# x lands in z instead of a ring of buffers, and a rearranged last stage: wavelet, convolution and median on one NeuronCore

## Time and profile before

| | us |
|---|---|
| median of 3 runs | 419.66 (417.89 to 421.17) |
| the profiled execution | 418.86 |
| its span, first to last instruction | 417.1 |
| TensorE matmuls busy | 396.9 (95%) |
| VectorE busy | 375.6 (90%) |
| GpSimd busy | 190.8 (46%) |
| ScalarE busy | 152.9 (37%) |
| DMA moved | 26.72 MB, mean 64 GB/s |

### The profile page before, as it was taken

How to read it: one execution, slowest core, us unless ns; L and a number is a source line. 1 busy time by engine, 2 the same in 40 slices (tenths; PEclk the granted TensorE clock), 3 DMA queues, 4 the chain that set the end, 5 groups by cost and what they waited for, 6 DMA issues and landing times.

```text
span 417.1 us, 3651 instructions
## 1 busy us (share of the span) xinstructions
PE 396.9 (95%) x1120; PEld 210.5 (50%) x1120; DVE 375.6 (90%) x532; ACT 152.9 (37%) x348; POOL 190.8 (46%) x194
## 2 busy tenths in 40 slices
PE   7889999999999999999999999999999998699983
PEld 2335588856444444444444444444446787564331
DVE  3899857999849999999999998989989999999993
ACT  2565753412262432323241414141424222229902
POOL 3999395622624443445454343434343520006620
PEclk9999999999999999999999999999999999889995
DMA  8970200100101011010101001010100000002673
GB/s 301 410 320 3 95 6 2 50 0 2 51 0 50 4 47 52 0 50 0 50 2 51 27 23 50 3 50 0 51 0 2 0 1 2 0 0 116 282 282 127
DMA packets 7796, 26.72 MB, mean 64 GB/s; under 512 B 992, under 2 KB 1248, under 8 KB 7776
## 3 DMA queue, kind: packets, MB, share of 16 engines
q1 hardware_dynamic: 7776, 26.48, 16.7%
HBM read 18.09 MB, written 8.39 MB: 63 GB/s over the span
## 4 chain that ended last, share of the span: by engine, by line
PE 71%; DVE 13%; POOL 5%; ACT 5%; issue 3%; DMA 2%; SPq 0%; POOLq 0%; DVEq 0%
PE conv_ps L381 65%; ACT z L618 3%; PE one_ps L363 3%; PE one_ps L446 2%; POOL y L212 2%; POOL y L213 2%; DMA ru<-x 2%; PE conv_ps L469 1%; POOL y L340 1%; DVE one_ps L821 1%; DVE sorted_cols L792 1%; DVE sorted_cols L794 1%; DVE sorted_cols L790 1%; DVE sorted_cols L787 1%; DVE z L823 1%
## 5 line engine op out<-in xcount | busy, mean ns | idle before, releaser
L381 PE MATMUL conv_ps<-ru,wt 128*128 128x512 f32 (+1 forms) x360 | 133.7, 509 | 0.0
L381 PEld LDWEIGHTS conv_ps<-ru,wt 128*128 128x128 f32 x360 | 69.9, 195 | 53.9 <-issue 50.2
L381 PE MATMUL conv_ps<-xu,wt 128*128 128x496 f32 (+3 forms) x240 | 88.6, 506 | 5.6 <-DVE conv_ps L757 5.6
L569 ACT ACTIVATE y<-conv_ps,sgn 128x512 f32<-128x512 f32 (+1 forms) x40 | 25.5, 637 | 171.0 <-PE conv_ps L381 171.0
L381 PEld LDWEIGHTS conv_ps<-xu,wt 128*128 128x128 f32 x240 | 46.0, 193 | 42.0 <-issue 33.2
L319 POOL TENSOR_TENSOR ru<-eo 128x512 f32<-128x512 f32 x16 | 17.0, 1061 | 86.5 <-DVE one_ps L785 86.4
L219 POOL TENSOR_TENSOR ru<-z 128x512 f32<-128x512 f32 x14 | 18.1, 1290 | 59.4 <-DVE one_ps L827 59.4
L381 PE MATMUL conv_ps<-ru,v 128*128 128x496 f32 (+3 forms) x120 | 43.7, 500 | 0.0
L381 PE MATMUL conv_ps<-y,wt 128*128 128x496 f32 (+3 forms) x108 | 38.6, 491 | 0.0
L381 PE MATMUL conv_ps<-y,v 128*128 128x496 f32 (+3 forms) x108 | 38.6, 491 | 0.0
L469 PE MATMUL conv_ps<-z,w 128*128 128x512 f32 x64 | 31.2, 637 | 4.8 <-POOL z L349 4.3
(11 more groups left out here) (128 smaller groups left out, 639.8 us busy)
## 6 DMA issues: line engine op xcount, KB each, us to landing
raw<-x SPq DMA_DIRECT2D x20, 512.0 KB, 3.3
out<-y SPq DMA_DIRECT2D x15, 512.0 KB, 2.6
ru<-x SPq DMA_DIRECT2D x8, 512.0 KB, 8.7
xu<-x SPq DMA_DIRECT2D x4, 512.0 KB, 8.7
wt<-w_t SPq DMA_DIRECT2D x2, 576.0 KB, 10.6
out<-y SPq DMA_DIRECT2D x2, 256.0 KB, 2.1
w<-w_t SPq DMA_DIRECT2D x2, 64.0 KB, 4.7
vec<-vectors SPq DMA_DIRECT2D x1, 3.0 KB, 9.5
```

The lines of the kernel that those rows point to most:

```text
L381: return nc.tensor.matmul(bank(u, b)[:, (r0 - row) * BW:(r1 - row) * BW], taps(half, kx, ky), plane[:, (r0 + dy) * BW:(r1 + dy) * BW], sta ...
L569: S.activation(at(slot(n), row * W + b, [[2, cols]]), src, ACT.Identity, scale=sgn[:, :], accum_out=y_sum[:, part:part + 1]).then_inc(y_ke ...
```

## The change

- x is loaded straight into `zslot(n)`, the place of the image's bands in `z`. The ring is gone, each image has a semaphore of its own, and SyncE issues all 16 loads with no wait. The vectors and weights stay behind the eighth. All waits that guarded the ring's buffers go.
- The seeds of unit 18 move from the piece of unit 16 to the end of the piece of unit 15; those of unit 19 from the piece of unit 17 to the piece of unit 16.
- The batch norm stands behind step 7 of the last three pieces (units 17, 18, 19).
- Images 3, 6, 9 and 12 (`SUMMED`) are finished without VectorE: ScalarE maps `y` with ReLU, TensorE adds it through an identity matrix (`unit`) onto the mix, and ScalarE writes PSUM + b as output. The other twelve (`OWN`) are mapped by GpSimd and finished by VectorE; nine of them stand behind steps 16, 19, ... 40 of the last three pieces, the others behind the last piece.
- GpSimd builds the identity after its last `make_xu03`. `KEEP_WARM` is 30.

```
-    WARM_UP, KEEP_WARM = 8, 24
-    RING = 8
+    WARM_UP, KEEP_WARM = 8, 30
...
-    BN3_AT, FINISH_AT = 8, tuple(range(15, 29))
-    ACT_SHARE = 1
+    SUMMED = (3, 6, 9, 12)
+    OWN = [n for n in range(IMAGES) if n not in SUMMED]
+
+    BN3_AT, FINISH_AT = 7, (16, 19, 22, 25, 28, 31, 34, 37, 40)
...
-        ring = [raw[0], raw[1], ru03[0], ru03[1], ru12[1], ru12[0], xu03[1], xu03[0]]
+        unit = sb("unit", [CH, CH])
...
         def make_xu12(v, n):
-            src = ring[n % RING]
-            e, o = at(src[:, :], 0, [[2, HALF]]), at(src[:, :], 1, [[2, HALF]])
+            e, o = at(zslot(n), 0, [[2, HALF]]), at(zslot(n), 1, [[2, HALF]])
...
-            for n in range(RING):
-                sp.dma_start(ring[n][:, :], x_img[:, n, :]).then_inc(x_in[n], 16)
-            sp.dma_start(vec[:, :], vectors).then_inc(vec_in, 16)
-            for half in (X_HALF, R_HALF):
-                cols = slice(half * KY * KX * CH, (half + 1) * KY * KX * CH)
-                sp.dma_start(wt[:, cols], w3_cols[:, cols]).then_inc(w3_in[half], 16)
-            for n in range(RING, IMAGES):
-                sp.wait_ge(x_in[n - RING], 16)
-                wait_xu12(sp, n - RING)
-                sp.dma_start(ring[n - RING][:, :], x_img[:, n, :]).then_inc(x_in[n - RING], 16)
+            for n in range(IMAGES):
+                sp.dma_start(zslot(n), x_img[:, n, :]).then_inc(x_in[n], 16)
+                if n == 7:
+                    sp.dma_start(vec[:, :], vectors).then_inc(vec_in, 16)
+                    for half in (X_HALF, R_HALF):
+                        cols = slice(half * KY * KX * CH, (half + 1) * KY * KX * CH)
+                        sp.dma_start(wt[:, cols], w3_cols[:, cols]).then_inc(w3_in[half], 16)
...
             for n in range(IMAGES):
-                if n < 2:
-                    sp.wait_ge(x_in[n], 32)
-                    wait_xu12(sp, n + RING)
-                else:
+                if n >= 2:
...
+            G.memset(unit[:, :], 1.0).then_inc(ones_set, 1)
+            pool.wait_ge(ones_set, 1)
+            G.affine_select(out=unit[:, :], in_=unit[:, :], pattern=[[-1, CH]], base=0, channel_multiplier=1,
+                            compare_op=ALU.is_equal, fill=0.0).then_inc(unit_made, 1)
...
-                    mm = nc.tensor.matmul(conv_ps[:, k, b * BANK:(b + 1) * BANK], w2[:, :], zslot(n)[:, b * BANK:(b + 1) * BANK],
-                                          start=True, stop=True)
+                    half = slice(b * BANK, (b + 1) * BANK)
+                    mm = nc.tensor.matmul(conv_ps[:, k, half], w2[:, :], zslot(n)[:, half], start=True, stop=n in OWN)
+                    if n in SUMMED:
+                        pe.wait_ge(x1_by_act, SUMMED.index(n) + 1)
+                        mm = nc.tensor.matmul(conv_ps[:, k, half], unit[:, :], slot(n)[:, half], start=False, stop=True)
...
+            for n in range(1, IMAGES):
                 norm_median(n)
-                if n % 4 >= 4 - ACT_SHARE:
-                    map_x1(n)
+                if n in SUMMED:
+                    S.activation(slot(n), slot(n), ACT.Relu, bias=shift3[:, :], scale=scale3[:, :]).then_inc(x1_by_act, 1)
+                if n - 2 in SUMMED:
+                    act.wait_ge(mix_done, n - 1)
+                    S.activation(slot(n - 2), conv_ps[:, n % 2, :], ACT.Identity, bias=cb2).then_inc(out_by_act, 1)
...
+            EARLY, LATE = {}, {}
+            for u in range(2, len(UNITS)):
+                before = EARLY if UNITS[u - 2][0] in HALVED or UNITS[u][0] in HALVED else LATE
+                before[u - 2] = u
+            last = len(UNITS) - 1
+            del EARLY[last - 3], EARLY[last - 2]
+            LATE[last - 4], EARLY[last - 3] = last - 1, last
...
-            medians(PIECES[-2:], step_and_more)
+            medians(PIECES[-3:], step_and_more)
```

More of the change, by code:

```diff
@@ L82, in wavelet_conv_median_kernel @@
         ru03 = [sb(f"ru03_{k}", [CH, PIX]) for k in range(2)]
-        ring = [raw[0], raw[1], ru03[0], ru03[1], ru12[1], ru12[0], xu03[1], xu03[0]]
-        assert len(ring) == RING
         UP = BW + 1
@@ L124, in wavelet_conv_median_kernel @@
         tmp1, tmp2 = one_ps[:, 0, :], one_ps[:, 1, :]
-        x_in = [sem(f"x_in{k}") for k in range(RING)]
+        x_in = [sem(f"x_in{n}") for n in range(IMAGES)]
         raw_in = [sem(f"raw_in{k}") for k in range(2)]
@@ L183, in wavelet_conv_median_kernel @@
         mix_done = sem("mix_done")
+        ones_set = sem("ones_set")
+        unit_made = sem("unit_made")
+        out_by_act = sem("out_by_act")
         out_ready = sem("out_ready")
@@ L249, in _ @@
             for n in range(IMAGES - 1):
-                sp.wait_ge(out_ready, n + 1)
+                if n in SUMMED:
+                    sp.wait_ge(out_by_act, SUMMED.index(n) + 1)
+                else:
+                    sp.wait_ge(out_ready, OWN.index(n) + 1)
                 sp.dma_start(out_img[:, n, :], slot(n)).then_inc(out_sent, 16)
             for part in range(2):
-                sp.wait_ge(out_ready, IMAGES + part)
+                sp.wait_ge(out_ready, len(OWN) + part)
                 half = slice(part * HALF, (part + 1) * HALF)
@@ L279, in _ @@
             for n in BY_POOL:
-                pool.wait_ge(x_in[n % RING], 16 * (n // RING + 1))
+                pool.wait_ge(x_in[n], 16)
                 make_xu12(G, n).then_inc(xu12_by_pool, 1)
@@ L313, in make_ru03 @@
                 pool.wait_ge(eo_made, n + 1)
-                if n < 2:
-                    wait_xu12(pool, 2 + RING + n)
-                else:
+                if n >= 2:
                     pool.wait_ge(rows_read, last_unit(n - 2) + 1)
@@ L349, in _ @@
                 G.memset(at(zslot(n), 0, [[(H - 1) * W, 2], [W - 1, 2]]), 0.0).then_inc(med_ready, 1)
-                if n % 4 < 4 - ACT_SHARE:
+                if n in OWN:
                     map_x1(n)
@@ L478, in _ @@
             pe.wait_ge(w2_in, 16)
+            pe.wait_ge(unit_made, 1)
             pe.wait_ge(squares_summed, PARTS_ALL)
@@ L482, in _ @@
             for n in range(2, IMAGES):
-                pe.wait_ge(out_ready, n - 1)
+                if n - 2 in SUMMED:
+                    pe.wait_ge(out_by_act, SUMMED.index(n - 2) + 1)
+                else:
+                    pe.wait_ge(out_ready, OWN.index(n - 2) + 1)
                 mix(n, n % 2)
@@ L541, in x_edges @@
                 act.wait_ge(raw_in[k], 16 * (n // 2 + 1))
-                if n < 2:
-                    wait_xu12(act, IMAGES - 1 - n)
-                else:
+                if n >= 2:
                     act.wait_ge(y_done, 2 * (last_unit(n - 2) + 1))
@@ L618, in norm_median @@
                 S.activation(zslot(n), zslot(n), ACT.Relu, bias=shift3[:, :], scale=scale3[:, :]).then_inc(med_normed, 1)
-            def map_x1(n):
-                S.activation(slot(n), slot(n), ACT.Identity, bias=shift3_bias2[:, :], scale=scale3[:, :]).then_inc(x1_by_act, 1)
-            for n in range(1, 4):
+            for n in range(1, IMAGES):
                 norm_median(n)
-            for n in range(4 - ACT_SHARE, 4):
-                map_x1(n)
-            for n in range(4, IMAGES):
-                norm_median(n)
-                if n % 4 >= 4 - ACT_SHARE:
-                    map_x1(n)
+                if n in SUMMED:
+                    S.activation(slot(n), slot(n), ACT.Relu, bias=shift3[:, :], scale=scale3[:, :]).then_inc(x1_by_act, 1)
+                if n - 2 in SUMMED:
+                    act.wait_ge(mix_done, n - 1)
+                    S.activation(slot(n - 2), conv_ps[:, n % 2, :], ACT.Identity, bias=cb2).then_inc(out_by_act, 1)
         @block.vector
@@ L651, in split_x @@
             def split_x(n):
-                dve.wait_ge(x_in[n % RING], 16 * (n // RING + 1))
+                dve.wait_ge(x_in[n], 16)
                 make_xu12(V, n).then_inc(xu12_by_dve, 1)
@@ L731, in _ @@
                 step(V.memset(at(t, 0, [[PITCH, H + 1]]), LOW))
-            for n in range(2):
-                wait_xu12(dve, RING + 5 - n)
             for k, (normed, made) in enumerate(((first_pair_normed, first_sums_made), (bands_normed, ru12_made))):
@@ L757, in seed_odd, with median @@
                 V.tensor_tensor(q_bank, p_kept[u % 2][:, 0:cols], q_bank, ALU.subtract).then_inc(seeded, 1)
-            def median(n, kept, pair0=0, pairs=BH, step=step, seeds=None):
-                early, late = (seeds, None) if n in HALVED or n + 2 in HALVED else (None, seeds)
+            def median(n, kept, pair0=0, pairs=BH, step=step, early=None, late=None):
                 r0, nr = 2 * pair0, 2 * pairs
@@ L855, in _, with medians @@
                 done_pairs = upto
-            def medians(pieces, step=step, seeds=None):
+            EARLY, LATE = {}, {}
[5 more added lines that the diff above has]
+            LATE[last - 4], EARLY[last - 3] = last - 1, last
+            def medians(pieces, step=step):
                 for n, pair0, pairs, u in pieces:
```

(12 more changed lines are left out.)

4 lines of the change are left out of this document (1 added, 3 removed).

## The result

The changed kernel takes 417.11 us in the median of 20 runs, against 419.51 us for the kernel before, also of 20. The ratio is 0.9947, with a 95% interval from 0.9932 to 0.9961: faster by half a per cent, within the one per cent that I called no change. Two of the 20 runs took 608 and 863 us, for a reason that no kept trace shows; the ratio leaves them out.

A forecast was written before the change was run, and what follows sets the result against it. TensorE fills the convolution; VectorE's order, waiting about 3 us for TensorE's mixes, ends the kernel. Tail end 413.5 plus 0.3 for handovers gives span 413.8, profiled time 415.6, median 416.4, stated as 416.6 us; range 412.6 to 420.3.

The forecast's parts named there:

- x into z costs and brings nothing: First pass: loading x without the ring is worth 0, at worst a loss of 1 us, no gain.
- Seeds one piece earlier: Convolution's end: TensorE's pauses of 2.30 and 3.28 us vanish; unit 18 runs to 357.9 us, unit 19 to 363.1.
- Statistics: Piece of unit 17: VectorE waits 1.1 us, then works 2.4 us, to 366.7; batch norm ready 9.3 us earlier.
- what ends the kernel is VectorE's own order: Last stage: the batch norm comes 9.3 us earlier, but VectorE's own sequence of work sets the kernel's end.
- Five finishes fewer, and TensorE's 20 mixes: Last stage: last median at 402.6 us without waits; about 3 us of waits for TensorE make it 405.7, against 407.99.
- ScalarE's outputs at no cost: Last stage: ScalarE's four outputs fit beside TensorE's mixes, value 0; upper bound 0.8 us in all.
- Tail: After the last median: end at 414.8 us with the last mix at half clock, 412.8 at full; 413.5 taken.
- Rival A: Full gain: TensorE keeps its clock in the tail, VectorE waits less; times 412.5 to 415.6 us; chance 0.27.
- Rival B: No gain: TensorE's clock falls in pauses ahead of images 2 and 3, costing 1.8 us; time 419.2; chance 0.15.
- Rival C: Slower: weight changes for the sums cost TensorE 0.2 us per added matmul, 3.3 us; time 420.5; chance 0.08.
- Rival D: First pass loses image 8's margin, 1 us; chance 0.05 together with the unseen.

The follow-up runs named there:

- e8: Changed kernel with 11 warm-up matmuls in place of 8 ahead of the first image; ratio to the kernel before 0.9935.
- e1: Kernel before with only x's loads into z (no ring, none of its waits), last stage old; ratio to the kernel before 0.9997.
- e2: Changed kernel with the ring and its waits put back, last stage new; ratio to the kernel before 0.9915.
- e3: Changed kernel with SUMMED empty: early seeds and statistics stay, VectorE finishes all 16 images; ratio to the kernel before 1.0015.
- e4: Changed kernel with its four sums, but statistics back behind step 8 of unit 18's piece, later finishes, 62 keep-warm matmuls; ratio to the kernel before 0.9984.
- e6: Changed kernel with its nine finishes at earlier steps (12 to 38) and 22 keep-warm matmuls; 414.26 us, ratio to the kernel before 0.9885.
- e9: Changed kernel with earlier finishes, 22 keep-warm and 11 warm-up matmuls, image 14's mix made twice; 412.27 us, ratio to the kernel before 0.9827.
- e5: Changed kernel with three sums (images 4, 8, 12) in place of four and ten finishes behind steps 16 to 43; ratio to the kernel before 0.9936.
- e7: Changed kernel with the mix of image 14 made twice onto the same PSUM half; ratio to the kernel before 0.9939.

## Why the prediction was right

I said 416.6 us and no change within one per cent; it is 417.1. The forecast was a span 3.3 us shorter, and the mean spans differ by 3.0. The profiled execution itself came out 2.5 us longer than its forecast, 416.3 for 413.8, because the first mix and the last both ran at half clock in it. That the runs' median is only 0.5 us off owes something to luck: it hangs on how often the clock is low at these two places, and I had priced one of them with a middle value and the other not at all. In e8's profile, where neither is slow, the span is 413.6. Step by step:

- *x into z costs and brings nothing.* Right in the spans: e1, and e2 beside the changed kernel, differ from their partners by 0.2 us and by nothing. GpSimd's split of image 8 came at 19.59 us, 19.46 before. I hadn't counted the time around the span, which grew from 1.87 us in the mean to 2.35. It is 2.05 in e1 and 1.78 in e2, 1.99 to 2.46 in the others without a ring. So part of it seems to come with the new loads (eight more semaphores, for one), but no run takes that apart, and it stays open.
- *Seeds one piece earlier.* Right within 0.4 us: 15.2 us from the sums' start to the end of unit 19 (348.71 to 363.93), forecast 15.6.
- *Statistics.* Right: a wait of 1.11 us (1.1), 2.4 us of work. e3 shows that this alone is worth nothing, as the step "what ends the kernel is VectorE's own order" has it. e4 adds what I had not priced: with the sums it is worth some 2 us.
- *Five finishes fewer, and TensorE's 20 mixes.* Both sizes hold. Image 3's mix started 1.7 us later than forecast (379.37 for 377.7), and the last median ended at 407.7, 2.0 us later than 405.7. Of both, 1.2 us is the first pass (0.2 of it was won back by the first finish). Another 0.7 is a single step of the median, L781, right behind the first finish: the next instruction starts 0.97 us after it (375.48 to 376.45), where the like step at 373.99 takes 0.30. The trace shows no wait in it, and the cause stays open. In e8's profile, whose first pass isn't late, the same step is as long and the last median ends at 406.7. That VectorE loses 3 us to TensorE is borne out by e6, where nearly all of those waits are gone: its median ends at 403.4, 4.3 us sooner than in the changed kernel's profile and 3.1 sooner once that one's late first pass is taken off.
- *ScalarE's outputs at no cost.* Right: one takes 1.0 us. ScalarE idles 7.0 us ahead of the first and 1.2 ahead of each of the other three, waiting for TensorE, and TensorE has no gap behind the start of image 3's mix in which it could wait for them.
- *Tail.* I took 413.5 between full and half clock. No profile shows that: the pause of 2.3 us ends at half clock in the changed kernel's (3.60 us for the mix) and at full clock in those of e2 and e8 (1.95). A value between the two suits a mean over runs by luck; a fall 1.2 us into the mix, the mechanism that I gave, appears in none of them. The 3.7 us behind the last mix were 3.3 (412.99 to 416.3).
- *Rival A* didn't come: only one of the 18 times lies under its 415.6 us, and VectorE waited as counted. Its other condition, no wait of VectorE, nearly holds in e6 and e9, and e9's span is 410.0 where A had 409.7. *Rival B*: the pauses before images 2 and 3 were 1.61 and 1.77 us, and the clock held in the profiled execution. *Rival C* is refuted: the matmuls of the sums follow each other every 0.43 us.
- *Rival D* didn't come: image 8's split had no wait.
- *Unforeseen:* the slow first mix, in three of the eleven profiles here. In them the first pass ends at 44.9 to 45.3 us, in the others at 44.1 to 44.6.

The Trainium skill, "TensorE: Matmul & The Clock Gate", section "HAM oscillation — how this bites in real kernels", allows TensorE longer pauses than any of these at full clock. The traces differ: half clock after 2.28 us in the changed kernel and after 2.88 in e6, full clock after 2.29 in e2. Over all eleven profiles, behind the first pass: the clock held after every pause up to 2.04 us (the longest in e5, ahead of image 2). After 2.28 to 2.30 us it was lost twice (unit 18 before, the changed kernel's tail) and held three times (e2, e8, unit 18 in e1). It was lost at every one of 2.88 us and more. That is few pauses, and what else decides isn't shown.

## What to carry to other kernels

Work taken off the engine whose order sets the end is worth its duration only while the engine that takes it over has that time free; count the receiver's chain from its first release, and start that chain as early as its inputs allow (e6 won 3 us by placement, with eight keep-warm matmuls fewer). An earlier result is worth nothing until the engine that ends the kernel waits for it (e3 against e4). Where a pause of TensorE of more than 2 us stands ahead of the last matmuls, try to fill it by repeating work that is already there, if a PSUM bank can be rewritten harmlessly (e9).

## What the runs showed of the hardware

- A pause of TensorE of 2.3 us was followed by half clock in the changed kernel's profile and by full clock in those of e2 and e8, which have the same last stage. The changed kernel's runs form two groups by mean clock (10 and 8 of 18), 1.8 us apart in mean span.
- After eight warm-up matmuls on zeros and a pause of 1.1 to 1.5 us, the first four matmuls took 3.6 to 3.8 us in three profiles, and 1.95 where the timelines of the others show four by themselves (e3, e4, e6, e7), while the record of the granted clock says 1.00 throughout. It says 1.00 during the warm-up as well, whose matmuls take 0.45 us, twice the 0.22 of the keep-warm ones. For the first 10 us the durations are to be read, not that column.
- A 128 × 128 select took GpSimd 0.29 us and its memset 0.20:

```profile
337.91 0.29 POOL L335 TENSOR_SCALAR_AFFINE_SELECT unit<-unit 128x128 f32<-128x128 f32 x1
```

- ScalarE took 1.01 us to move 1024 columns from PSUM to SBUF with a bias, and 1.13 to map 1024 columns from SBUF to SBUF, start to start (383.11 to 384.12, and 384.12 to 385.25):

```profile
383.11 1.12 ACT L630 ACTIVATE y<-conv_ps,vec 128x1024 f32<-128x1024 f32 x1 [7.01 <-PE conv_ps L472]
384.12 1.23 ACT L622 ACTIVATE z<-z,shift,scale 128x1024 f32<-128x1024 f32 x1
```
